# An embedding, attention and mixture-of-experts block on one core: four neighbouring tokens per partition, second-layer weights loaded chunk by chunk, and closing loads that wait for the tiles with tokens

## The reference

```
h = patches(x) @ W + b                                   # 11776 x 128
h = h + attention(layernorm(h))                          # 8 heads; v and the scores, softmax
    # ax (sequence, head, feature, token), reread as rows of 1024 values, times Wlt (1024 x 128)
t = layernorm(h)
gates = softmax(t @ Wr + br); the two largest of 8, scaled to sum 1
out = h + sum over the two chosen e of gate_e * (relu(t @ W1[e] + b1[e]) @ W2[e] + b2[e])
```

## Time and profile before

| | |
|---|---|
| median of three runs | 1611.85 us |
| profiled execution, its own time | 1610.05 us |
| its span, first to last instruction | 1608.3 us |
| busy: PE, DVE, ACT, POOL | 1446.5, 1166.0, 1019.5, 826.4 us |
| mean granted clock of PE, share of full speed | 0.953 |
| moved by DMA | 247.37 MB, mean 154 GB/s |

### The profile page before, as it was taken

The page is one execution under the profiler, slowest core; times in us unless marked ns, Lnnn a source line. Parts: engine busy times, 40 slices in busy tenths (PEclk is TensorE's granted clock), DMA queues, the critical chain, the costliest instruction groups (busy, mean ns, idle before and its releaser), DMA issues.

```text
span 1608.3 us, 32773 instructions
## 1 busy us (share of the span) xinstructions
PE 1446.5 (90%) x8062; PEld 1157.2 (72%) x8062; DVE 1166.0 (73%) x3018; ACT 1019.5 (63%) x2282; POOL 826.4 (51%) x925
## 2 busy tenths in 40 slices
PE   4999999999999999999997899989939999999920
PEld 3677777777777777777775777768738888888820
DVE  1889898898988889888893577766726666666632
ACT  1677777777777777777774576766615555555510
POOL 1575334443344434444334677766745665665655
PEclk8999999999999999999999899998959999999965
DMA  3322222122221222222237566666446777677658
GB/s 79 130 71 100 77 80 85 70 100 76 82 84 71 96 78 84 82 73 91 82 121 269 182 216 246 221 214 217 163 175 240 245 247 253 239 251 250 238 178 297
DMA packets 128847, 247.37 MB, mean 154 GB/s; under 512 B 15376, under 2 KB 78496, under 8 KB 128800
## 3 DMA queue, kind: packets, MB, share of 16 engines
q1 hardware_dynamic: 97520, 204.34, 35.9%
q0 software_dynamic: 15008, 34.34, 6.5%
q10 hardware_dynamic: 16272, 8.15, 1.7%
HBM read 100.78 MB, written 90.43 MB: 119 GB/s over the span
## 4 chain that ended last, share of the span: by engine, by line
PE 63%; DVE 10%; issue 9%; ACT 8%; POOL 4%; DMA 4%; SPq 1%; ACTq 0%; POOLq 0%; DVEq 0%
PE bank L321 14%; PE bank L323 12%; PE bank L322 12%; PE bank L1361 6%; PE bank L1294 5%; PE bank L1386 3%; PE bank L1426 3%; DMA hch<-h_scratch 2%; POOL sorted_scratch L696 2%; PE bank L1435 2%; PE bank L1513 2%; PE bank L1538 1%; ACT xT L748 1%; DVE cent L1049 1%; DVE probT_l L1058 1%
## 5 line engine op out<-in xcount | busy, mean ns | idle before, releaser
L571 POOL TENSOR_TENSOR prob<-expo,inv 92x368 f32<-92x368 f32 x256 | 205.0, 801 | 458.2 <-DVE inv L1044 458.2
L723 POOL DMA_INDIRECT y_scratch<-ytok,tin x212 | 205.6, 970 | 154.2 <-DVE ytok L1246 88.9
L1237 DVE SCALAR_TENSOR_TENSOR hid_l<-bank,hid_h 128x512 fp32r<-128x512 f32 x212 | 146.7, 692 | 130.8 <-ACT hid_h L911 130.3
L696 POOL DMA_INDIRECT sorted_scratch<-trow,posi x184 | 180.9, 983 | 80.4 <-issue 56.2
L911 ACT ACTIVATE hid_h<-bank 128x512 fp32r<-128x512 f32 x212 | 127.0, 599 | 147.6 <-PE bank L323 147.6
L1361 PE MATMUL bank<-z,xnT 128*92 128x368 f32 x512 | 200.7, 473 | 0.2 <-ACT z L770 0.2
L770 ACT ACTIVATE z<-bank 128x368 f32<-128x368 f32 x256 | 122.1, 477 | 121.3 <-PE bank L323 118.5
L1037 DVE TENSOR_REDUCE peak<-bank 92x4 f32<-92x368 f32 x256 | 136.3, 532 | 71.2 <-PE bank L1361 69.1
L1030 DVE TENSOR_REDUCE total<-expo 92x4 f32<-92x368 f32 x256 | 133.6, 522 | 21.5 <-ACT expo L815 21.5
L1065 DVE TENSOR_TENSOR w2s<-bank,w2s 128x368 fp32r<-128x368 f32 x256 | 136.7, 534 | 11.6 <-ACT w2s L808 7.8
L815 ACT ACTIVATE expo<-cent 92x368 f32<-92x368 f32 x256 | 129.3, 505 | 24.2 <-DVE cent L1049 22.1
(11 more groups left out here) (187 smaller groups left out, 3872.6 us busy)
## 6 DMA issues: line engine op xcount, KB each, us to landing
ax_scratch<-val SPq DMA_DIRECT2D x64, 736.0 KB, 3.5
arow<-ax_scratch SPq DMA_DIRECT2D x23, 2048.0 KB
w1t<-w1s SPq DMA_DIRECT2D x53, 512.0 KB, 3.5
w2t<-w2s SPq DMA_DIRECT2D x53, 512.0 KB, 3.0
tin<-sorted_scratch SPq DMA_DIRECT2D x53, 260.0 KB, 3.0
xin<-in_x_dram SPq DMA_DIRECT2D x32, 372.0 KB
yin<-y_scratch SPq DMA_DIRECT2D x46, 256.0 KB, 4.5
h_scratch<-hT SPq DMA_DIRECT2D x32, 184.0 KB, 7.1
```

Source lines behind the costliest of these rows:

```text
L571: nc.gpsimd.tensor_tensor(prob[:, k % 2], expo[:, k % 2], inv[:, k % 2].unsqueeze(2).to_broadcast([S, HH, S]), ALU.mult).then_inc(prob_kep ...
L696: pool.indirect_dma_start(out=sorted_dram, out_offset=bass.IndirectOffsetOnAxis(ap=posi[:, q, choice, r:r + 1], axis=0), in_=trow[:, q, ch ...
L723: pool.indirect_dma_start(out=y_dram, out_offset=bass.IndirectOffsetOnAxis(ap=tin[:, b, r, D:D + 1].bitcast(I32), axis=0), in_=ytok[:, b % ...
L1237: V.scalar_tensor_tensor(hid_l[:, f], hid_ps[f][:], 0.0, hid_h[:, f].bitcast(F32), ALU.max, ALU.subtract).then_inc(hidl_kept, 1)
```

## The change

In the second stage a chunk's rows go to arow as "(p r)": partition p gets tokens 4p to 4p + 3, 16 KB in one piece. PE's turned columns then stand in the order r, p, so DVE reads hch with a stride of four elements. h1tok, the places and the output follow, and the store writes 2 KB for a partition. w2 is loaded by SP, one expert in each of chunks 0 to 7, behind that chunk's `load_a`; ACT and POOL split one expert in each of chunks 1 to 8. The spare tiles are written one in each of chunks 0 to 6. Chunks 1 to 8 are written out ahead of the loop.

In the closing, yin has eight slots. Four of them lie in arow's room, which the third stage doesn't use; the four slots of osb (outs) lie in the room of the first stage's weights for Wlt. The loads of chunks 0 to 3 wait for the scatters of the tiles with tokens only; their number comes out of one more PE matmul ahead of the table and four small DVE operations behind it (real). Chunk 4's loads wait for all scatters.

```
-FIN = 4
+FIN = 8
+FIRST = 4
+OUTS = 4
...
+        outs = sb("outs", [P, OUTS, RT, D], stack=closing)
...
-        yin = sb("yin", [P, FIN, 2, RT, D], stack=fourth)
-        osb = sb("osb", [P, FIN, RT, D], stack=fourth)
+        yroom = sb("yroom", [P, FIN - FIRST, 2, RT, D], stack=fourth)
+        yearly = raw.rearrange("p (s k r d) -> p s k r d", s=FIRST, k=2, r=RT)
+        yin = [yearly[:, s] if s < FIRST else yroom[:, s - FIRST] for s in range(FIN)]
...
-                sp.dma_start(arow[q][:], rows.rearrange("(r p) n -> p r n", p=P)).then_inc(a_in[q], 16)
+                sp.dma_start(arow[q][:], rows.rearrange("(p r) n -> p r n", p=P)).then_inc(a_in[q], 16)
...
                     load_a(c + 2, i + 1, q)
+                if isinstance(c, int) and c < NE:
+                    sp.dma_start(w2raw[:, c, :, 1], w2[c].rearrange("(c p) d -> p c d", p=P)).then_inc(ws_2[c], 16)
...
             tiles(sp, tile)
+            sp.wait_ge(real_kept, 2)
+            sent = [sp.value_load(real[0:1, half:half + 1], ...) for half in (0, 1)]
             for half in (0, 1):
-                sp.wait_ge(y_out[half], 16 * TR * ((TILES + 1 - half) // 2))
+                sp.wait_ge(y_out[half], sent[half])
...
                 at_least(sp, sum2_kept, c - FIN + 1)
+                if isinstance(c, int) and c == FIRST:
+                    for half in (0, 1):
+                        sp.wait_ge(y_out[half], 16 * TR * ((TILES + 1 - half) // 2))
...
-            for e in range(NE):
-                pool.dma_start(w2raw[:, e, :, 1], w2[e].rearrange("(c p) d -> p c d", p=P)).then_inc(ws_2, 16)
...
-                if isinstance(c, int) and c in (1, 2):
-                    for e in range(4 * c - 4, 4 * c):
-                        low_w(w2raw[:, e, :, 1], w2split[:, e, :, 0], w2split[:, e, :, 1], NE + e)
+                if isinstance(c, int) and 1 <= c <= NE:
+                    low_w(w2raw[:, c - 1, :, 1], w2split[:, c - 1, :, 0], w2split[:, c - 1, :, 1], NE + c - 1)
+                if isinstance(c, int) and c < SPARE:
+                    lay_spare(c)
...
-                V.tensor_tensor(h1[:, q], proj_ps[:], hch[q][:], ALU.add).then_inc(h1_kept, 1)
+                V.tensor_tensor(h1[:, q].rearrange("d (r p) -> d r p", r=RT), proj_ps[:].rearrange("d (r p) -> d r p", r=RT),
+                                hch[q][:].rearrange("d (p r) -> d r p", r=RT), ALU.add).then_inc(h1_kept, 1)
...
-                act.dma_start(out[sl, :].rearrange("(r p) d -> p r d", p=P), osb[:, q]).then_inc(out_sent[q], 16)
+                act.dma_start(out[sl, :].rearrange("(p r) d -> p r d", p=P), osb[q % OUTS]).then_inc(out_sent[q % OUTS], 16)
...
+            ins = mm(row_ps[:, 2 * TILES:3 * TILES], past[:, NE - 1:NE], ident[0:TILES, 0:TILES], start=True, stop=True)
             ins.then_inc(listed, 1)
```

More of the change, by code:

```diff
@@ L115, in build @@
         before = sb("before", [P, P])
+        closing = ExitStack()
+        outs = sb("outs", [P, OUTS, RT, D], stack=closing)
+        closing.close()
+        osb = [outs[:, s] for s in range(OUTS)]
         wlt_h = sb("wlt_h", [P, AC, D], F32R)
```

50 lines of the change are left out of this document (30 added, 20 removed).

## The result

The changed kernel takes 1592.28 us (median of 4 runs, 1590.38 to 1594.90), the kernel before 1611.17 us beside it (1609.23 to 1611.92). The ratio is 0.9886, with a 95% interval of 0.9869 to 0.9903. The profiled execution has a span of 1588.6 us against 1608.3, so 19.7 us to account for; what lies around the span is 1.8 us in both.

The account below looks back on a forecast made before the run. Full DMA engines bound the second stage's start, then POOL's sequence; DVE with POOL, DMA and output slots limited the closing. 10.5 + 0.8 - 0.25 + 9.4 = 20.4 us off 1610.05 gave 1589.6 profiled, median 1591.4, range 1583.5 to 1602.5.

Parts of the forecast that it names:

- Start: Start of the second stage: without w2's loads and the spare-tile burst, chunk 1's root comes 10.5 us sooner, bounds 4.4 and 13.
- POOL's extras: Second stage, chunks 1 to 8: single low_w and spare tiles cost POOL 7.7 us against 8.56, so 0.8 us gained.
- The strided add: Second stage, DVE's add reading hch with a stride: hidden, 0 us; at most 1.4 us an add, at worst 11 us lost.
- Closing: Closing: early loads and a pace of 1.92 us for 18 sums gain 9.4 us, between 6 and 11.5.
- Limit (b): Closing, DMA limit on the pace: with stores at the loads' rate a chunk takes 1.87 us.
- What was left in: Second stage: POOL's unexplained 4.22 us wait before a scatter, with 3 more behind it, assumed to stay; 0 us gained.
- rival 2: Second stage: POOL's unexplained stall goes with its eight w2 DMAs, 7 us more gained, 1584 us; chance 10%.
- 1 (only the closing gains): Second stage: chunks 1 and 2 still come late and spare tiles on POOL cost 5 us, 1601 us in all; chance 16%.
- 3 (pace of 2.04): Closing: the pace stays 2.04 us since eight chunks in flight delay the stores, 1593.6 us; chance 14%.
- 4 (slower, by the clock): Second stage, chunks 1 to 8: PE's idle drops its clock each time, costing 25 us, 1616 us; chance 4%.
- 5: Closing: without fillers the early loads wait like the others, 5 us less gained, 1596.4 us; chance 2%.
- the prediction's 2.8 us: Closing: most that could be lost if DVE's early adds held up POOL's four last scatters, 4 x 0.69 us.

## Why the prediction was right

The prediction was 1591.4 us, the measurement 1592.28. Point by point:

- **Start, 10.5 forecast, 8.9 measured.** Both waits went, and chunk 1's root came 29.6 us behind its load (28.0 forecast). The 1.6 us lie in PE's part: chunk 1 starts 11.5 us after the load's issue (10.4 forecast), chunk 2 11.2 later (11.1 forecast; the prediction calls these two chunks 0 and 1 there), and the root 6.9 behind that, not 6.5. The first 1.1 us are the clock. The forecast took chunk 0's part of PE from the trace of before, where it ran at 2.4 GHz; after, it began at 1.2 GHz and the twelve turns alone took 1.3 us more. The clock had fallen ahead of the stage, and not because of this change: the kernel with only the placing of tokens shows 2.80 us for these turns too, and two of the kernels built on the change show 1.51. From 864 on it was 2.4 GHz, as forecast. The prediction named w2's loads and the spare tiles together and put w2's first; that the spare tiles' burst is the larger part in the kernels with long rows, through chunk 2's wait, it did not see.
- **POOL's extras, 0.8 forecast, -0.6 measured.** A chunk takes 13.58 - 12.25 = 1.33 us more with both and 0.60 with a `low_w` alone (0.51 forecast). So a spare tile costs 0.73, not 0.6, as its issue takes 0.65 us and not 0.54. That is 9.2 in all where it said 7.7.
- **The strided add, 0.** It takes 1.07 us instead of 0.69, below the allowed 1.4, and PE waits 0.9 us for it in all. Hidden, as forecast; PE's waits on ACT's `aT_f` stand behind POOL's longer chunk.
- **The table**, 0.1 against 0.25.
- **Closing, 9.4 forecast, 7.7 measured.** The head is right to 0.2 us (7.3 us from last scatter to fifth sum; 7.1 forecast). The pace was mis-sized: 2.008, not 1.92. The term at fault is one pace for all 18 sums. The four chunks ahead are used up at once, and sums 6 and 8 wait for loads (1.96 and 1.22 us of idle), while the engines move only 343 GB/s in the mean from 1539 to 1547: these two gaps are 1.9 us longer than the rest. From the ninth sum on the pace is 1.905, a little better than forecast. Limit (b) was also set too low: the engines move 406 GB/s, so a chunk's 786 KB take 1.94 us and not 1.87.
- **What was left in, 0 forecast, 4.4 measured.** What the chunks 9 to 22 take over 13 x 12.25 us shrank from 6.7 to 2.3. In size this is a good half of rival 2, but no run shows why POOL stalls or that w2's DMAs have a part in it. The misses above (1.6, 1.4, 1.7, and 1.2 us in the first stage) are about cancelled by it: 5.9 lost against 4.4 here, 0.6 in the third stage and 0.2 at the table. So the sum is closer than its terms, and that is luck: with the stalls as they were the median would stand near 1596.7, inside the range but 5 us off.

The rivals: 1 (only the closing gains) fell with both PE waits. 3 (pace of 2.04) holds in its number for the mean, but not for its reason: stores land in 5.5 us, the loads are late. 4 (slower, by the clock) fell: the pauses of 1.5 to 1.8 us in chunks 2 to 7 came, and the granted clock is 1.00 from 880 to 1060 us. 5 fell: the early loads go out 8.5 us ahead. Of the prediction's own signs, one that it called wrong came, a pace over 2.0 (2.008), and one that it expected didn't, stores landing in under 5 us (5.5).

The Trainium skill's "SBUF — State Buffer" (SBUF: two separate sides), by which VectorE with two SBUF inputs and GpSimd lock each other out and the one that starts first has the port for its whole instruction, was weighed for DVE's early adds holding up POOL's scatters. In the changed kernel's profile this price was not paid: the scatter at 1534.12 takes 0.97 us, as all do, and the next starts 0.30 behind it, beside an add at 1534.59. But there no scatter began while an add ran. Where one does, it is nearly always held up, and the other runs show it nineteen times. These are two rows of the run with w2's loads at the start:

```profile
1656.34 0.69 DVE L1292 TENSOR_TENSOR outs<-arow,h1tok 128x512 f32<-128x512 f32 x1 [1.47 <-DMA arow<-y_scratch]
1656.39 1.48 POOL L741 DMA_INDIRECT y_scratch<-ytok,tin  x1 [0.31 <-issue]
```

Such a scatter ends 0.84 or 0.85 us after the add's end each time and takes 1.02 to 1.48 us in place of 0.97. In that run three of the last four were held up, for 1.2 us in all. So the prediction's 2.8 us was a bound on something real, and the changed kernel's profile missed it by the accident of where its adds fell. Where DVE's add meets POOL's sums, the 4.41 us agree with the lock, but not with this order: the add's start stands 0.15 us ahead of the first sum's, and it ended behind the third.

## What to carry to other kernels

Where two transfers meet on full engines, look at the issue times and packet sizes of all of them, not only at the one that was named: the burst that hurts may be the second, and small packets beside large ones are what falls back. Before a stretch is taken over from the old trace into a forecast, read the clock that it ran at. Size a ring of buffers together with the packet size of what shares the queues; without long rows, slots and early loads brought 1.7 us of 7.7. And see how long after an engine's last instruction the program ends: giving GpSimd's last few adds to VectorE gained more than most steps of this change.

## What the runs showed of the hardware

- The span ends 8.5 us behind GpSimd's last instruction when this comes last, with DMA silent for over 6 us of it. It ends 2.6 us behind the end of VectorE's last add when GpSimd was done 7 us earlier.
- A VectorE add of 128x512 f32 from PSUM and SBUF takes 692 ns, and 1074 ns where the SBUF operand is read with a stride of 16 bytes.
- A VectorE add caught beside three GpSimd adds in a row took 4.41 us, all of their time.
- A GpSimd scatter (DMA_INDIRECT) that starts while a VectorE add with two SBUF inputs has over 0.1 us left to run ends 0.84 to 0.85 us after the add: nineteen of them, in eight kernels, took 1.02 to 1.48 us instead of 0.97. One that started 0.04 us behind an add was not held up.
- Stores of 512-byte rows beside loads for eight slots land in 8.1 us, 2 KB rows in 5.5; both kinds of transfer then move 24.1 KB per engine-us, 512-byte rows 18.7 to 18.8 (2.13 / (0.355 x 320)).
- The kernel before takes 1611 us on one chip and 1728 to 1747 on others; the start of the second stage lies at about the same time and the closing is as long on all. On those others engines of all kinds stop for up to 5 us in the second and third stages, and the mean granted clock is lower. Why is open.
